# Attention on four 32-row ranges of TensorE in place of stacks built by DMA, with one table of PSUM banks and new orders

## The reference

```python
x = x + _L0_xattn_ref(_layernorm(x), ctx_768, ...)   # 16 heads of 8 features, 77 keys, with biases
x = x + _L0_ffn_ref(_layernorm(x), ...)              # fake-quantized gate/up/down, width 352
x = x + _L1_xattn_ref(_layernorm(x), ctx_768, mask, ...)
x = x + _L1_ffn_ref(_layernorm(x), ...)              # 8 experts of width 256, all computed, gelu, summed, x a gate
```

```python
q = (x @ Wq).reshape(B, N, 16, 8);  k, v = context @ Wk, context @ Wv
attn = softmax(where(mask, q k^T * 8 ** -0.5, max_neg), axis=-1)
out = (attn @ v).reshape(B, N, 128) @ Wo
```

## Time and profile before

| | us |
|---|---|
| median of 3 runs | 354.68 |
| lowest, highest of them | 347.61, 355.9 |
| the profiled execution | 349.38 |
| its span, from first to last instruction | 347.6 |
| busy in the span: PE, PEld | 297.2, 216.3 |
| DVE, ACT, POOL | 226.1, 198.3, 159.9 |
| moved by DMA | 19.20 MB, of it 4.95 MB read from HBM |
| mean granted TensorE clock | 0.906 |

### The profile page before, as it was taken

One profiled execution on the slowest core, in us unless ns is written; L12 is line 12 of the kernel. 1 busy time (PEld: TensorE's weight loads), 2 busy tenths in 40 slices (PEclk: granted clock), 3 DMA queues, 4 the chain that ended last, 5 costly groups with the idle time before them and its releaser, 6 DMA issues.

```text
span 347.6 us, 5091 instructions
## 1 busy us (share of the span) xinstructions
PE 297.2 (85%) x1537; PEld 216.3 (62%) x1537; DVE 226.1 (65%) x599; ACT 198.3 (57%) x334; POOL 159.9 (46%) x223
## 2 busy tenths in 40 slices
PE   3777779899987796468698998999999999999995
PEld 1476355665563783457475466865668787787774
DVE  5949638943842478899887178993457755664462
ACT  5100844386656167271215546677778888888892
POOL 6889686325131498604873604666512430700000
PEclk9995669969999989686756899999999999999999
DMA  8958144105002410220640324000000000000000
GB/s 227 194 135 180 45 115 106 41 2 144 2 8 46 106 19 3 64 58 2 165 108 8 72 74 115 23 9 10 0 3 0 2 30 1 0 32 1 0 32 30
DMA packets 15736, 19.20 MB, mean 55 GB/s; under 512 B 6174, under 2 KB 9779, under 8 KB 15703
## 3 DMA queue, kind: packets, MB, share of 16 engines
q1 hardware_dynamic: 9756, 10.55, 12.1%
q0 software_dynamic: 5136, 7.22, 9.3%
q10 hardware_dynamic: 818, 1.10, 1.2%
HBM read 4.95 MB, written 1.05 MB: 17 GB/s over the span
## 4 chain that ended last, share of the span: by engine, by line
PE 42%; DVE 8%; DMA 2%; issue 2%; POOL 2%; ACT 1%; SPq 1%; DVEq 0%; ACTq 0%; POOLq 0%
PE ps_y L1248 4%; PE ps_fun L1236 4%; PE ps_y L1250 4%; PE ps_y L1249 4%; PE ps_fun L1237 4%; PE ps_fun L1238 4%; PE ps_fun L1136 4%; PE ps_tok L1126 3%; PE ps_pv L1146 2%; POOL lq L557 2%; PE ps_misc L1093 1%; DMA qst<-mthl 1%; DVE hbuf L939 1%; DVE hbuf L940 1%; DVE mx L829 1%
## 5 line engine op out<-in xcount | busy, mean ns | idle before, releaser
L612 ACT ACTIVATE p<-ps_fun 117x512 f32<-117x512 f32 (+1 forms) x88 | 49.0, 594 | 24.5 <-PE ps_fun L1136 23.6
L922 DVE TENSOR_TENSOR hhl<-hf,hhl 128x512 fp32r<-128x512 f32 x64 | 43.4, 690 | 27.5 <-ACT hf L680 26.7
L679 ACT ACTIVATE hhl<-ps_fun,b 128x512 fp32r<-128x512 f32 x64 | 44.2, 690 | 19.2 <-PE ps_fun L1238 13.7
L829 DVE TENSOR_REDUCE mx<-ps_tok 128x6 f32<-128x468 f32 (+1 forms) x80 | 44.8, 589 | 11.9 <-PE ps_tok L1126 11.5
L1136 PE MATMUL ps_fun<-qst,kst 103*117 103x512 f32 (+1 forms) x88 | 42.6, 519 | 5.0 <-ACT p L612 3.5
L1126 PE MATMUL ps_tok<-kst,qst 97*128 97x234 f32 (+1 forms) x160 | 38.1, 351 | 7.2 <-DMA qst<-qhi 3.4
L680 ACT ACTIVATE hf<-ps_fun,b 128x512 f32<-128x512 f32 x64 | 44.0, 688 | 0.0
L1126 PEld LDWEIGHTS ps_tok<-kst,qst 97*128 97x128 f32 x160 | 30.4, 236 | 15.3 <-DVE mx L829 6.5
L458 POOL DMA_DIRECT2D qst<-mthl x48 | 24.8, 524 | 30.8 <-DVE mthl L877 30.2
L440 POOL TENSOR_SCALAR veps<-mv 128x4 f32<-128x4 f32 x16 | 4.2, 264 | 66.4 <-DVE mv L735 66.0
L1136 PEld LDWEIGHTS ps_fun<-qst,kst 103*117 103x117 f32 (+1 forms) x88 | 16.8, 202 | 23.4 <-ACT p L612 15.3
(11 more groups left out here) (206 smaller groups left out, 641.1 us busy)
## 6 DMA issues: line engine op xcount, KB each, us to landing
qst<-qhi SPq DMA_DIRECT2D x90, 64.0 KB, 2.6
qst<-qlo POOLq DMA_DIRECT2D x48, 64.0 KB, 2.8
kst<-karea SPq DMA_DIRECT2D x15, 87.8 KB
x<-in_x SPq DMA_DIRECT2D x4, 256.0 KB, 8.2
w1raw<-in_w POOLq DMA_DIRECT2D x1, 1024.0 KB, 11.5
w2raw<-in_w POOLq DMA_DIRECT2D x1, 1024.0 KB, 6.8
...
```

The source lines that it names most:

```text
L612: act.activation(p[0:w, j, :], fun[f_of["key", u, j]][0:w, :], ACT.Exp, scale=SCALE).then_inc(q["p_ready"], 1)
L679: act.activation(hh[:, b % HR, :], fun[f_of["w1", 0, b]][:, :], ACT.Gelu, bias=b1[:, b % NH:b % NH + 1])
L829: nc.vector.tensor_reduce(mx[:, u % 2, t, 2 * HG * pair:2 * HG * pair + w, 0], bank[:, 0:w * MP].rearrange("p (h j) -> p h j", h=w), AX.X, ...
L922: nc.vector.tensor_tensor(hl[:, b % HR, :], hf[:, b % HF, :], hh[:, b % HR, :].bitcast(F32), ALU.subtract).then_inc(q["h_lo"], 1)
```

## The change

- **Rows.** Heads are in four groups of four; group r has its 32 query features on partitions 32r to 32r + 31, which is where the projection puts them. No stack is built: `qst`, `kst`, `mthi`, `mthl` and all copies from SBUF to SBUF are gone.
- **Scores.** A token job covers 128 tokens and all heads: for each of the four row ranges matmuls with K = 32 and 312 columns (4 heads x 78) into a bank of its own, one pass for each product (three in layer 0, four in layer 1 with the mask), accumulated in PSUM: 12 or 16 matmuls, 4 jobs a sample. A key job is a chunk of 117, 117 or 78 of the 312 key columns: four passes of four matmuls of 512 columns, 3 jobs a sample. A job holds four banks.
- **Maxima and exponentials.** DVE reduces two banks with one instruction (8 of 616 columns a sample), ACT makes the exponential of two banks with one (6 of 1,024 columns a sample). The maxima are split on DVE before the transpose into pairs on the partitions 32r + 0 to 7, with a one in row 8 for the mask, and ACT copies them once (`mt`).
- **Keys and values.** Layer 0's keys are widened by ACT and DVE straight from PSUM, layer 1's by POOL (`keys_widened`), which makes the mask rows too (`mask_rows`). A value job has three matmuls of 128 columns where it had two of 192. `pvb` has four outputs in place of three.
- **Banks.** All eight banks are one tensor. Each PE job names its banks in the table (`tok.0.0@6723`), and before it uses a bank PE waits for whatever read it last.
- **Orders.** All tables are new. The value jobs of layer 0 stand ahead of `xt.0`; POOL loads and splits w1 and w2 in layer 0 and moves no rows; the layer norm is applied by ACT for the first norm only (`LN_ACT = [0, 1, 2, 3]`), by DVE for the others. `FILL` is shorter: in attention of layer 1 16 matmuls of ones where there were 45, and none ahead of `lg` and `y`, where there were 5.

The core of the diff:

```diff
-LN_ACT = {2, 3, 4, 5, 6}
+LN_ACT = [0, 1, 2, 3]
...
     (0, "PE"): """
+        kt.0@0 vr0.0@1 vr0.1@2 vr0.2@3 vr0.3@4 xt.0@1 kt.1@5 q.0@4 xt.1@1 tok.0.0@6723 tok.0.1@0145 tok.0.2@6723 q.1@0 tok.0.3@4567 tok.1.0@2301
+        max.0@6 tok.1.1@4523 key.0.0@6701 tok.1.2@4523 xt.2@6 vr.0@7 key.0.1@0145 tok.1.3@2367 q.2@0 key.0.2@2345 pva.0@1 tok.2.0@6723 xt.3@0
...
     (0, "POOL"): """
+        lnstat.0 lnstat.1 lnstat.2 mxset.0 bias.0 loads.0 lnstat.3 w1split.0 w2split.0 kt.0 kmx.0 wo.0 bias.1 bias.2 wo.1 bias.3 wo.2 wo.3 hclear.0
...
+    {('kt', 0, 0): 14, ('xt', 0, 0): 5, ('q', 0, 0): 2, ('tok', 0, 0): 4, ('nt', 3, 0): 12, ('gate', 0, 0): 12, ('gate', 3, 0): 2, ('gate', 6, 0): 3,
+     ('gate', 10, 0): 4, ('gate', 11, 0): 4},
+    {('down', 0, 0): 9, ('down', 1, 0): 3, ('xt', 0, 0): 2, ('q', 0, 0): 2},
...
-                        for g in range(G):
-                            r = slice(ROW0[g], ROW0[g] + SR)
-                            move(qst[0:SR, u % 2, g, :], qhi[r, u % 2, :], stack_q[u % 2][g])
-                            if u > 0:
-                                move(qst[SR:2 * SR, u % 2, g, :], qhi[r, u % 2, :], stack_q[u % 2][g])
...
+                        for half in range(2):
+                            act.activation(p[0:w, j, 2 * half:2 * half + 2, :], pair_of("key", u, j, half)[0:w], ACT.Exp, scale=SCALE).then_inc(q["p_ready"], 1)
...
+                        for half in range(2):
+                            heads = pair_of("tok", u, j, half)[:, :, 0:KR].rearrange("p r (h j) -> p r h j", h=HR4)
+                            nc.vector.tensor_reduce(mxr[:, u % 2, j, 2 * half:2 * half + 2, :], heads[:, :, :, 0:M], AX.X, ALU.max).then_inc(q["tok_maxed"], 1)
...
+                        link(nc.vector.tensor_copy(two[:, :, :, 0].bitcast(F32R), full))
+                        nc.vector.tensor_tensor(two[:, :, :, 1], full, two[:, :, :, 0], ALU.subtract).then_inc(q["mx_split"], 1)
...
+            def score_banks(job, u, j, name, count):
+
+                four = at[job, u // B, u % B, j]
+                for n in four:
+                    freed(n)
+                for i, n in enumerate(four):
+                    owner[n] = (name, count + i // 2)
...
+                        banks = score_banks("tok", u, j, "tok_maxed", 2 * (NT * u + j) + 1)
+                        pe.wait_ge(q["q_lo"], u + 1)
...
+                        for r in range(R):
+                            rows = slice(32 * r, 32 * r + 32)
+                            mm(banks[r][:, 0:KR], qhi[rows, u % 2, cols], kbd[rows, L, 0, b, :], start=True, stop=False)
+                        for r in range(R):
+                            rows = slice(32 * r, 32 * r + 32)
+                            mm(banks[r][:, 0:KR], qhi[rows, u % 2, cols], kbd[rows, L, 1, b, :], start=False, stop=False)
...
+                        for r in range(R):
+                            rows = slice(32 * r, 32 * r + 32)
+                            shifts = kmx0[rows, cols] if L == 0 else kmx1[rows, b, cols]
+                            ins = mm(banks[r][0:w, :], shifts, mt[rows, u % 2, :], start=False, stop=True)
+                        ins.then_inc(q["key_put"], 1)
```

More of the change, by code:

```diff
@@ L20 @@
 H, HD = 16, 8
[L22 to L25, removed]
+R, HR4 = 4, 4
+KR = HR4 * MP
+CHUNKS = [(0, 117), (117, 117), (234, 78)]
+NC = len(CHUNKS)
 PR = 117
[L28 to L40, removed]
+MASKROW = 2 * HR4
 CP = 112
@@ L51 @@
 HF = HR = 4
-LN_ACT = {2, 3, 4, 5, 6}
+LN_ACT = [0, 1, 2, 3]
+LN_POOL = []
 H_POOL = [5, 8]
@@ L58 @@
 EPS32 = float(np.finfo(np.float32).eps)
-CW = 128 + HG + 1 + 2 + 64
+FOLD = R * HD + R
+CW = 128 + HR4 + 1 + 2 + FOLD
 ORDERS = {
     (0, "PE"): """
[L64 to L70, removed]
-        pvb.3 on.3 ot.3 wo.3 nt.3
@@ L352, in xn_wait @@
                 engine.wait_ge(q["xn_act"], sum(k <= n for k in LN_ACT))
+            elif n in LN_POOL:
+                engine.wait_ge(q["xn_pool"], sum(k <= n for k in LN_POOL))
             else:
-                engine.wait_ge(q["xn_dve"], sum(k <= n for k in range(4 * B) if k not in LN_ACT))
+                engine.wait_ge(q["xn_dve"], sum(k <= n for k in range(4 * B) if k not in LN_ACT and k not in LN_POOL))
         def h_wait(engine, n):
@@ L1130, in attention @@
                     if job == "key":
[L1131 to L1136 removed]
+                        lo, w = CHUNKS[j]
@@ new lines, in attention @@
+                        cols = slice(lo, lo + w)
+                        banks = score_banks("key", u, j, "p_ready", 2 * (NC * u + j) + 1)
+                        pe.wait_ge(q["mt_copied"], u + 1)
+                        pe.wait_ge(q["kmo_in"], 16)
+                        for r in range(R):
+                            rows = slice(32 * r, 32 * r + 32)
+                            mm(banks[r][0:w, :], kbd[rows, L, 0, b, cols], qhi[rows, u % 2, :], start=True, stop=False)
+                        for r in range(R):
+                            rows = slice(32 * r, 32 * r + 32)
+                            mm(banks[r][0:w, :], kbd[rows, L, 1, b, cols], qhi[rows, u % 2, :], start=False, stop=False)
@@ new lines, in attention @@
+                        for r in range(R):
+                            rows = slice(32 * r, 32 * r + 32)
+                            mm(banks[r][0:w, :], kbd[rows, L, 0, b, cols], qlo[rows, u % 2, :], start=False, stop=False)
+                        for r in range(R):
+                            rows = slice(32 * r, 32 * r + 32)
+                            shifts = kmx0[rows, cols] if L == 0 else kmx1[rows, b, cols]
+                            ins = mm(banks[r][0:w, :], shifts, mt[rows, u % 2, :], start=False, stop=True)
```

815 lines of the change are left out of this document (330 added, 485 removed).

## The result

| | before | after |
|---|---|---|
| median of the runs, us | 352.44 (4 runs) | 314.34 (4 runs) |
| lowest, highest | 347.61, 355.9 | 313.16, 317.41 |
| span of the profiled execution | 347.6 | 315.6 |
| busy: PE, PEld | 297.2, 216.3 | 269.1, 192.7 |
| DVE, ACT, POOL | 226.1, 198.3, 159.9 | 219.2, 199.8, 104.6 |

The ratio of the times is 0.902 with a 95% interval of 0.889 to 0.916: faster by 10%. Forecast were 317 us within 300 to 345. Runs over 1.5% above the fastest of their kernel count as slow: ratios leave them out, medians and spreads hold them.

The account below looks back on a forecast made before the run. No engine limits the whole: PE bounds the stage after 200 us, while layer 0 and layer 1's opening pay for stacks. 347.6 - 22 (layer 0) - 10 (layer 1) = 315.6 us span, so 317 us; range 300 to 345.

Parts of the forecast that it names:

- 17.3 and 28 predicted: Start of layer 0: first token matmul at 17.3 us against 25.3, first key matmul at 28 against 40.3.
- 4.4 booked: Opening of layer 1: 5.3 us of copies after the query go, one 0.8 us DVE subtraction replaces them.
- 6.6 booked: Layer 1, first token to first key matmul: rest of the 11 us gain at the first key beyond 4.4.
- 0.3 for the changes of a job: PE, each token or key job: changing between row ranges and full array costs 0.3 us, bounds 0.1 and 0.5.
- +9: PE, token and key jobs: over eight samples PE has 9 us more work than before.
- The fills it had set against that, -8: PE, layer 1: tables lose 34 fills, or 68 instructions at 0.117 us, 8 us less work.
- PE's work is about the same; the gain is from starting earlier and waiting less: PE, whole kernel: 9 us more job work stands against 8 us fewer fills; matmuls get no cheaper.
- so it is covered by 10 us: Layer 0: POOL's new work ends at about 50 us, DVE reaches wo.0 only at about 60.
- The feed-forward: Feed-forward of layer 0, after its attention: unchanged at 37 us.
- A: Rival, token and key jobs: row ranges don't run together, 123 us more, about 430 us; chance 0.07.
- B: Rival, token and key jobs: matmuls overlap but weight loads don't, 42 us more, about 352 us; chance 0.12.
- C (banks late): Rival, layer 1 after 200 us: held banks delay w1 and w2, up to 1 us a job, 345, likelier 331; chance 0.13.

Follow-up runs that it names:

- e8: Kernel before without the copies of queries and maxima into the query stack, its tables and key stacks kept: 351.7 us, ratio to before 0.999.
- e3: Changed kernel with twelve query copies a sample put back as a cost, the sample's first token job waiting for them: 372.1 us, 1.058 to before.
- e4: Changed kernel with six copies of the maxima a sample put back as a cost, the first key job waiting for them: 350.0 us, 0.993 to before.
- e2: Kernel before with 34 fills (68 matmuls) fewer, in layer 1 and in front of lg.3 and y.3 in layer 0: 352.6 us, ratio 1.006.
- e9: Changed kernel with POOL's weight splits cut into eight pieces each and its clearing of h0 into four: 307.5 us, ratio to before 0.881.

## Why the prediction was right, and where it was not

The time was right (317 against 314.3), and so was what the rows of a job and of the openings would look like. That the span hit the sum to the tenth (315.6) is luck: by stages the sum was off by 3.7, 1.2 and 2.5 us, and terms in it were wrong against each other.

**What goes.** The opening of layer 0 was right to half a microsecond: 17.3 and 28 predicted, 16.82 and 27.81 measured. In layer 1, from the second whole maximum to the first token matmul it takes 20.4 us instead of 25.5: 5.0 gained, 4.4 booked. From there to the first key matmul 13.0 us instead of 15.9: 2.9 gained, 6.6 booked. The step that failed is the working that added up DVE's four token jobs and little else; in the trace the second sample's query stands in between at half clock (2.01 us from 149.77) and its tokens ahead of the first keys (at 156.88). The reasoning that the copies cost what PE is seen to wait for them was incomplete: by e8 the removal alone brings 6.8 us at its best milestone, and by e3 and e4 it is the licence for the new tables. The prediction's milestones contained that, since they were worked out from the new tables.

**PE's price of a job.** Of 0.17 a round, 0.14 came (312 columns), of 0.235 0.233, of 0.3 for the changes of a job 0.29: 0.19 behind its first start (1.12 less 4 x 0.233) and the 0.10 ahead of it. A token job between full matmuls costs 0.74 us in layer 0 and 0.88 in layer 1 (predicted 0.81 and 0.98), a key job 1.22 (1.24). A sample is then at most 4 x 0.74 + 3 x 1.22 = 6.6 us in layer 0 and 7.2 in layer 1, against 6.2 before, and less where jobs of row ranges follow each other without a change: in eight samples between nothing and 6 us are added, where the sum had +9. The fills it had set against that, -8, gave nothing either (e2), and their 34 are 29 in layer 1 and the 5 ahead of lg and y in layer 0. Two errors of opposite sign.

**Waiting or working.** "PE's work is about the same; the gain is from starting earlier and waiting less" isn't what the busy times say. PE's idle time fell by 3.9 us only (50.4 to 46.5), its busy time by 28.1: by 12.0 ahead of the first whole maximum and by 12.5 between the second one and the first w1 matmul (59.3 to 46.7). 66 fewer fill instructions at 0.117 us are 7.7 of it. Busy time also holds the stretching at the lower clock (rounds of 512 columns are 0.43 us apart at 158 us, where 0.50 was granted), so waiting less can show as shorter busy time; how much of the 28 us is which wasn't taken apart.

**The end of layer 0.** 99 predicted, 103.5 measured. The term that failed is "so it is covered by 10 us": POOL's new work was weighed only by when POOL would be finished, and there it is indeed covered. What it does meanwhile to DVE's SBUF operations was not asked, and it cost PE 5.1 us and the clock behind it (e9: 92.2). A row of the trace before could have told; it wasn't among those read:

```profile
122.65 1.80 POOL L517 MEMSET hbuf<- 32x2048 f32 x1
...
123.15 1.58 DVE L1000 TENSOR_SCALAR xn<-xn,rqs 128x512 f32<-128x512 f32 x1
```

The same DVE operation takes 0.49 us in the trace after; here it ends 0.28 us behind POOL's clearing.

**The feed-forward** was to stay and gave 1.2 us (21.2 instead of 22.4 between the maxima). POOL's weight split of the earlier trace rows ran in this stage before and no longer does; that it is the cause wasn't tested.

**The rest.** From the first key to the first w1 matmul of layer 1 2.4 us were gained, from there to the end 2.2, where nothing was booked. By stages: -18.3 (predicted -22), -1.2 (0), -12.5 (-10), in sum -32.0.

**Rivals.** A and B are refuted by the rounds. C (banks late) didn't show where it was expected: in the stage after w1 PE is busy 125.6 of 127 us, and the key matmuls' waits for ACT's exponentials are 3.2 us over the whole kernel. Ahead of w1 token matmuls do wait for DVE's reductions, 8.7 us in six waits, of which 5.1 are POOL's stall.
